# Last inverse transform of a four-layer spectral kernel: row transposes replaced by row products over 32 partitions

## The reference, cut to what matters

```python
x = x + _L0_conv_ref(_gn(x), L0_conv_weights_r, L0_conv_weights_i)
x = x + _L1_conv_ref(_gn(x), L1_conv_gain)
x = x + _L2_conv_ref(_gn(x), L2_conv_weight)
x = x + _L3_conv_ref(_gn(x), L3_conv_weights)
```

```python
x_f = jnp.fft.rfft2(x)
k_f = jnp.fft.rfft2(weights)
out_f = jnp.einsum('bchw,ochw->bohw', x_f, k_f)
out = jnp.fft.irfft2(out_f, s=(H, W))
```

## Time and profile before

| | |
|---|---|
| median of 3 runs | 964.11 us |
| profiled execution, its own time | 966.74 us |
| its span, first to last instruction | 965.0 us |
| granted TensorE clock over the span, mean | 0.933 of full |
| PE busy | 783.1 us (81%) |
| DVE busy | 599.2 us (62%) |
| ACT busy | 517.2 us (54%) |
| POOL busy | 122.3 us (13%) |
| the replaced stage | from about 868.5 us to the end |

### The profile page before, as it was taken

How to read it: one execution, slowest core, us unless ns; L and a number is a source line. 1 busy time by engine, 2 the same in 40 slices (tenths; PEclk the granted TensorE clock), 3 DMA queues, 4 the chain that set the end, 5 groups by cost and what they waited for, 6 DMA issues and landing times. The chain is left out here.

```text
span 965.0 us, 27107 instructions
## 1 busy us (share of the span) xinstructions
PE 783.1 (81%) x10775; PEld 654.0 (68%) x10775; DVE 599.2 (62%) x1112; ACT 517.2 (54%) x868; POOL 122.3 (13%) x120
## 2 busy tenths in 40 slices
PE   5999997872599565787599999985888488979998
PEld 5999996762488443666444444434777488979997
DVE  2454454775847599588777777676666677742222
ACT  0132236863453272565379999004887657765564
POOL 0000000100010054255202222000000100001110
PEclk9999998996899889799799999997999789999999
DMA  6399868542000100000000000004000448831222
GB/s 279 150 373 336 316 203 227 141 98 73 3 1 0 32 9 0 2 0 0 0 2 1 1 1 1 1 1 105 1 0 0 87 89 177 178 81 44 100 106 99
DMA packets 44553, 80.08 MB, mean 83 GB/s; under 512 B 19130, under 2 KB 37568, under 8 KB 40656
## 3 DMA queue, kind: packets, MB, share of 16 engines
q1 hardware_dynamic: 27856, 62.48, 22.7%
q10 hardware_dynamic: 16640, 16.78, 5.1%
HBM read 50.74 MB, written 27.92 MB: 82 GB/s over the span
## 5 line engine op out<-in xcount | busy, mean ns | idle before, releaser
L1473 DVE SCALAR_TENSOR_TENSOR X<-bank,c_power,X 32x512 f32 x128 | 96.8, 757 | 36.4 <-PE bank L1423 32.8
L925 DVE TENSOR_TENSOR X<-X,bank 128x512 f32 x64 | 43.6, 682 | 92.3 <-PE bank L911 92.3
L1616 PE MATMUL bank<-m_xp,m_kf 128*32 128x64 f32 x2048 | 81.6, 246 | 21.9 <-DVE m_xp L1551 10.4
L1616 PEld LDWEIGHTS bank<-m_xp,m_kf 128*32 128x32 f32 x2048 | 80.6, 171 | 23.2 <-issue 23.1
L429 ACT COPY ks_spec<-bank 128x512 f32<-128x512 f32 x64 | 34.3, 589 | 104.1 <-PE bank L357 101.3
L411 DVE COPY ks_rows<-bank 128x512 f32<-128x512 f32 x64 | 41.2, 686 | 72.5 <-PE bank L342 72.5
L215 DVE BATCH_NORM_STATS2 bn<-X 128x6 f32 x128 | 83.1, 683 | 2.9 <-POOL X L1213 1.6
L342 PE MATMUL bank<-ks_fw,ks_src 64*128 64x64 f32 x1024 | 68.7, 298 | 11.4 <-DMA ks_src<-in_L_conv_weights 11.4
L1379 ACT ACTIVATE c_r<-X,c_nrm 32x1024 f32 (+1 forms) x56 | 75.2, 1343 | 2.4 <-DVE c_nrm L1447 1.1
L342 PEld LDWEIGHTS bank<-ks_fw,ks_src 64*128 64x128 f32 x1024 | 68.1, 215 | 11.4 <-issue 11.4
L357 PE MATMUL bank<-ks_fh,ks_rows 64*128 64x128 f32 (+1 forms) x1152 | 72.6, 281 | 0.2 <-ACT ks_spec L429 0.2
(11 more groups left out here) (189 smaller groups left out, 1854.1 us busy)
## 6 DMA issues: line engine op xcount, KB each, us to landing
ks_src<-in_L_conv_weights SPq DMA_DIRECT2D x8, 2048.0 KB, 8.2
kf<-ks_spec ACTq DMA_DIRECT2D x16, 1024.0 KB, 8.7
m_kf<-kf SPq DMA_DIRECT2D x32, 512.0 KB, 8.0
X<-in_x SPq DMA_DIRECT2D x4, 2048.0 KB, 13.7
out_y<-X SPq DMA_DIRECT2D x16, 512.0 KB, 2.6
l_wb<-in_L_conv_weights_r SPq DMA_DIRECT2D x4, 512.0 KB, 11.0
l_wb<-in_L_conv_weights_i SPq DMA_DIRECT2D x4, 512.0 KB, 13.7
xf<-f_xm SPq DMA_DIRECT2D x4, 448.0 KB
```

The lines of the kernel that those rows point to most:

```text
L925: dve.tensor_tensor(x, x, ps[4 + c % 4][:], ALU.add).then_inc(added, 1)
L1473: dve.scalar_tensor_tensor(x, of.rearrange("p (y x) -> p y x", x=HN), filt.power[at, 2:3], x, ALU.mult, ALU.add).then_inc(added, 1)
L1616: last = pe.matmul(ps[4 * half + m // 8][at:at + C, m % 8 * N:(m % 8 + 1) * N], kf[p][:, j, :, H * half + m], xp[half][:, j, m].rearrange( ...
```

## The change

`inverse_stage` is replaced for the last layer by `l3_inverse_stage`, which has no loops and no staging:
- `turn`: 128 transposes read `xm` itself, with a step of 16 elements (64 bytes). VectorE and ScalarE take turns (`turned_by`) in copying four of them at a time to `cols`
- `first_slot`: four small products treat slot 0 (with `l3_first`, which replaces `l3_ih0`), copied back into `cols` by VectorE; then all columns use the one matrix `mh`
- `columns`: 128 products, to banks 0 to 3; results go to `t`, which lies in the memory of `xm`. 20 of the 32 copies are VectorE's, 12 ScalarE's (`made_by`). One product now takes the 4 x 32 columns of all image groups' slots as its stationary operand, so that its result has the slots on the partitions
- pixels: no transposes. For each image row and each of real and imaginary part there are four products, each over 32 partitions (one image group q each), 128 columns of `t` as the stationary operand and 64 moving columns, to bank 4 * (c % 2) + q; real and imaginary part are summed in PSUM. That is 8 chunks of 64 products. VectorE adds four banks to `X` for a chunk, and SyncE stores 256 KB for each, 32 stores in all.

```diff
--- before.py
+++ after.py
@@ -91,7 +91,7 @@
     iw = np.stack([np.cos(ang * np.outer(s, n)), -np.sin(ang * np.outer(s, n))], 1) * 2 / N
     iw[0, 0] = 1.0 / N
     iw[0, 1] = (-1.0) ** n / N
-    out["l3_iw"] = two(iw[sum(SLOT_AT, [])].reshape(2 * SLOT, N))
+    out["l3_iw"] = np.tile(iw[sum(SLOT_AT, [])], (Q, 1, 1)).reshape(P, 2 * N)
     f0 = np.zeros((N, 2, N, 2))
@@ -106,7 +106,7 @@
                 f0[:, half, at, 0], f0[:, half, at, 1] = 1.0, (-1.0) ** n
                 i0[at, 0, :, half], i0[at, 1, :, half] = 1.0 / N, (-1.0) ** n / N
     out["l3_fh0"] = f0.transpose(0, 1, 3, 2).reshape(P, P)
-    out["l3_ih0"] = i0.reshape(P, P)
+    out["l3_first"] = i0.reshape(P, P) @ np.linalg.inv(out["l3_ih"])
     k = np.arange(PS)
@@ -953,6 +953,146 @@
                         if g >= 4:
                             act.wait_ge(pixels, NCH * q + (g - 3) * 4 // per)
                         act.copy(tt[g % 4][:], ps[g % 4][:]).then_inc(turned2_read, 1)
+def l3_inverse_stage(pr, xm, mats):
+    nc, ps = pr.nc, pr.psum
+    SG = SLOT // 4
+    turned, first, first_read, made, pixels, added, stored = (pr.sem(f"i3_{n}") for n in (
+        "turned", "first", "first_read", "made", "pixels", "added", "stored"))
+    turned_read, made_read = ([pr.sem(f"i3_{n}{e}") for e in range(2)] for n in ("turned_read", "made_read"))
+    turned_by = [a % 2 for a in range(SLOT)]
+    made_by = [1 if k % 8 in (1, 4, 7) else 0 for k in range(SLOT)]
+    out_groups = pr.out.rearrange("(q b) c h w -> q (b c) (h w)", b=IB)
+    mh, m0, mw = mats
+    with ExitStack() as ctx:
+        cols = pr.sb(ctx, "i3_cols", [P, IB, C, Q, SLOT])
+        t = xm[:].rearrange("p s k r b -> p (s k r b)").rearrange("p (r h m) -> p r h m", r=2, h=N)
+        def wait_read(eng, sems, by, n):
+            for e in range(2):
+                if e in by[:n]:
+                    eng.wait_ge(sems[e], by[:n].count(e))
+        with nc.Block() as block:
+            @block.sync
+            def _(sp):
+                for c in range(NCH):
+                    for q in range(Q):
+                        sp.wait_ge(added, Q * c + q + 1)
+                        at = slice(c * CH, (c + 1) * CH)
+                        sp.dma_start(out_groups[q][:, at], pr.X[:, q, at]).then_inc(stored, 16)
+                sp.wait_ge(stored, 16 * NCH * Q)
+            @block.tensor
+            def _(pe):
+                def turn(b):
+                    for a in range(SG * b, SG * b + SG):
+                        q, half = a % SG // 2, a % 2
+                        if a >= 4:
+                            wait_read(pe, turned_read, turned_by, a - 3)
+                        for s in range(4):
+                            m = pe.transpose(ps[a % 4][:, s * P:(s + 1) * P],
+                                             xm[:, 4 * half + s, :, :, IB * q + b].rearrange("p k r -> p (k r)"),
+                                             pr.ident[:])
+                        m.then_inc(turned, 1)
+                def first_slot(b):
+                    wait_read(pe, turned_read, turned_by, SG * b + SG)
+                    pe.matmul(ps[4 + b][:, 0:P], m0[:], cols[:, b, :, :, 0].rearrange("p o q -> p (o q)"),
+                              start=True, stop=True).then_inc(first, 1)
+                def columns(b):
+                    pe.wait_ge(first_read, b + 1)
+                    for k in range(SG * b, SG * b + SG):
+                        if k < 4:
+                            wait_read(pe, turned_read, turned_by, SLOT - 3 + k)
+                        else:
+                            wait_read(pe, made_read, made_by, k - 3)
+                        for o in range(4):
+                            m = pe.matmul(ps[k % 4][:, o * P:(o + 1) * P],
+                                          cols[:, b, 4 * (k - SG * b) + o].rearrange("p q s -> p (q s)"), mh[:],
+                                          start=True, stop=True)
+                        m.then_inc(made, 1)
+                turn(0)
+                for b in range(1, IB):
+                    turn(b)
+                    first_slot(b - 1)
+                columns(0)
+                first_slot(IB - 1)
+                for b in range(1, IB):
+                    columns(b)
+                wait_read(pe, made_read, made_by, SLOT)
+                for c in range(NCH):
+                    if c >= 2:
+                        pe.wait_ge(added, Q * (c - 1))
+                    for h in range(ROWS):
+                        for r in range(2):
+                            for q in range(Q):
+                                at = slice(q * SLOT, (q + 1) * SLOT)
+                                m = pe.matmul(ps[4 * (c % 2) + q][:, h * N:(h + 1) * N], t[at, r, ROWS * c + h],
+                                              mw[at, r * N:(r + 1) * N], start=r == 0, stop=r == 1)
+                    m.then_inc(pixels, 1)
+            def copy_turned(eng, copy, e, a):
+                if turned_by[a] == e:
+                    b, q, half = a // SG, a % SG // 2, a % 2
+                    eng.wait_ge(turned, a + 1)
+                    copy(cols[:, b, :, q, 16 * half:16 * half + 16].rearrange("p o (s k) -> p o s k", s=4),
+                         ps[a % 4][:].rearrange("p (s k o) -> p o s k", s=4, k=4)).then_inc(turned_read[e], 1)
+            def copy_made(eng, copy, e, k):
+                if made_by[k] == e:
+                    eng.wait_ge(made, k + 1)
+                    copy(t[:, :, :, 4 * k:4 * k + 4].rearrange("p r h o -> p h r o"),
+                         ps[k % 4][:].rearrange("p (o h r) -> p h r o", o=4, r=2)).then_inc(made_read[e], 1)
+            @block.vector
+            def _(dve):
+                def copy_first(b):
+                    dve.wait_ge(first, b + 1)
+                    dve.tensor_copy(cols[:, b, :, :, 0], ps[4 + b][:, 0:P].rearrange("p (o q) -> p o q", o=C)
+                                    ).then_inc(first_read, 1)
+                for b in range(IB):
+                    for a in range(SG * b, SG * b + SG):
+                        copy_turned(dve, dve.tensor_copy, 0, a)
+                    if b:
+                        copy_first(b - 1)
+                for k in range(SLOT):
+                    if k == SG:
+                        copy_first(IB - 1)
+                    copy_made(dve, dve.tensor_copy, 0, k)
+                for c in range(NCH):
+                    dve.wait_ge(pixels, c + 1)
+                    for q in range(Q):
+                        x = pr.X[:, q, c * CH:(c + 1) * CH]
+                        dve.tensor_tensor(x, x, ps[4 * (c % 2) + q][:], ALU.add).then_inc(added, 1)
+            @block.scalar
+            def _(act):
+                for a in range(SLOT):
+                    copy_turned(act, act.copy, 1, a)
+                for k in range(SLOT):
+                    copy_made(act, act.copy, 1, k)
@@ -1696,7 +1836,7 @@
         if stop == 2: return dump(pr)
         with ExitStack() as layer:
             xm = pr.sb(layer, "xm", [P, SLOT // 4, N, 2, B])
-            inv, inv_loads = matrices(pr, layer, [("l3_ih", [P, P]), ("l3_ih0", [P, P]), ("l3_iw", [P, P])])
+            inv, inv_loads = matrices(pr, layer, [("l3_ih", [P, P]), ("l3_first", [P, P]), ("l3_iw", [P, 2 * N])])
             with ExitStack() as inner:
                 kf0 = pr.sb(inner, "m3_kf0", [P, 2, C, N])
                 loaded = [pr.sem(f"m3_load{p}") for p in range(2)]
@@ -1704,7 +1844,7 @@
                 pr.stats_stage("n3", fwd_loads + inv_loads)
                 l3_forward_stage(pr, fwd, xm, kf0, loaded[0])
                 l3_mix_stage(pr, xm, kf0, loaded)
-            inverse_stage(pr, "i3", xm, SLOT, N, inv, 2, True)
+            l3_inverse_stage(pr, xm, inv)
 def dump(pr):
```

## The result

The changed kernel takes 960.08 us, the median of 15 executions (952.5 to 966.79), against 966.67 us for the kernel before on the same chip (961.53 to 969.58): a ratio of 0.9928 with a 95% interval of 0.9905 to 0.995. That is 0.7% faster where 1.4% was forecast. The profiled execution took 954.41 us with a span of 952.6, close to the 951.1 of the sum; the typical execution is some 6 us longer. The ratio leaves out executions more than 1.5% above the fastest (here one, of 966.79 us).

What follows compares the result with a forecast made beforehand. TensorE, busy almost without a break, was taken to bound the stage. Terms of 17.1 + 28.9 + 0.7 + 30.0 + 2.9 + 3.0 = 82.6 us save 13.9, giving 950.2 us; range 946.9 to 956.8, with starvation 946.5 to 962.

Steps and rivals of the forecast that it cites:

- The sum: Replaced stage: turning, columns, a wait, pixels, adds and last store add to 82.6 us, from 868.5 to 951.1 us.
- first uncertain step: Pixel products: four quarters go on independently past program order, starting four records every 0.112 us, 27.9 ns each.
- The serial rival: Pixel products: records start only behind their predecessors, 55.8 ns each, 57.1 us in all, median 977.3 us; chance 0.17.
- Phase C: Pixel products: 1024 records over 32 partitions in 30.0 us, 3.75 us a chunk, bounds 28.6 to 32.2 us.
- The allowance for the instruction blocks beside the stores: Pixel products: 0.2 us a chunk allowed for what the packet row can't show, giving 3.75 us a chunk.
- The reading of the earlier trace: Instruction blocks: a packet took 1.06 us in quiet, 0.96 us beside 359 GB/s, so the transfer doesn't suffer.
- The starvation rival: Pixel products: stores delay each instruction block to 5 us, making 40 us and a median of 960.2 us; chance 0.15.
- The tail: End of the stage: 0.13 us and four adds, 2.9 us, then 3.0 us from last add to end.
- Turning: Stage's first part: 128 transposes in 16.4 us plus three small first-slot products at 0.224 us, 17.1 us.
- The start: Stage's beginning: TensorE can start at 868.5 us once staging goes, with earlier layers untouched.
- The step that failed: Pixel products: full clock assumed throughout; a half-speed clock, listed as a sign of being wrong, would double the load-bound part.
- The forecast's base: Kernel before: median 964.11 us, from which 13.9 us was taken to give 950.2 us.

Runs made afterwards that it cites:

- the order by pairs: Changed kernel with only the order of its 512 pixel products altered, so neighbours use two quarters of the partitions, not four: 1016.4 us, pixel phase 94.2 us.
- after_f: Changed kernel, unaltered, one more single profile in search of a long execution: 965.73 us, pixel phase 43.3 us.
- the wide kernel: Changed kernel with each pixel product moving 128 columns instead of 64, the second 64 an overwritten copy: medians 956.43, 955.68 and 952.88 us in three sets.

## Why the prediction was wrong

*The sum* named its terms rightly. Its first uncertain step, that quarters go on independently past the program's order, held: four abreast, 0.112 us a step. The serial rival, to which 0.17 was given, is out, though the order by pairs shows what it would have meant.

*Phase C* was mis-sized by 2.0 us in the profiled execution, at the full clock: 32.0 us against 30.0. The allowance for the instruction blocks beside the stores, 0.2 us a chunk, was too small; in six other profiles of the kernel with the clock held the phase took 30.4 to 31.6 us from first to last record, and without stores 28.9 and 29.4. The reading of the earlier trace rows, that a block's packet takes no longer under load, was right but beside the point, since it shows the packet's transfer and not how long it queues. The starvation rival's mechanism is real at a tenth to a quarter of its price of 10 us (1.0 to 2.8 us). On this the Trainium skill ("Runtime: NRT & Kernel Launch", "Instruction fetch mechanics") says "mostly hidden"; 1.9 us of waits in 32 agrees with "mostly", at 28 ns a record. Of the stores, the 395 GB/s put in reach is 408 by its own row, 290 over 0.71; nothing hangs on it.

*The tail* was 6.3 us against 5.9: the adds ran in 2.5 us, but the last store landed later behind three others, 3.8 us from the last add to the end where 3.0 was reckoned.

*Turning* was 0.6 us longer than reckoned, and not for its transposes: all 128 took 16.3 us (9.07, 3.62 and 3.61) against the 16.4 of the sum. Two errors cancel there. The sum gave only the first sixteen transposes the half clock of the earlier trace rows, while in the kernel before the next eight column records still took 1.66 us instead of 0.89, and here the first 64 transposes took 1.8 us more than the rate of the later ones gives. But those came every 0.113 us instead of 0.120. What was mis-sized are the three small products: each held the engine for 0.45 us instead of 0.224. Why is not shown.

*The start* made 1.6 us of the 12.4 between the two profiles by chance. The changed stage itself went from 96.5 to 85.7 us, 10.8 us less, where 13.9 were forecast.

*The step that failed* is one that the sum put at nothing: the full clock through phase C. "A half-speed clock in phase C, which would double its load-bound part" stood among the signs of being wrong, with no chance and no price, and no reason was given for the zero. The rate of phase C came from products over 64 partitions that ran at a granted clock of 1.00; nothing in the trace before had a quarter of the rows. In after_f the clock fell to 0.50 after 14 us of the phase and cost 12 us. It or a shorter form of it is the likeliest cause of the 17 long executions of 49. That is argued and not shown for 16 of them, since only one was profiled; for it are the wide kernel's 0 of 18, and that the scatters of the kernel before and of the wide one are alike, 11.1 and 10.4 us. What sets a fall off is open, and so is why it comes in some executions only.

In the wide kernel, whose profiles show no fall, the median is 954.6 us, 1.1% under the 965.3 of the kernel before in the same three sets, near the forecast's 1.4%. By that comparison the falls take some 4.5 us of the median gain (959.1 less 954.6), an estimate with the chips mixed. The rest of the gap is in the stage at full clock: 3.1 us, of which 2.0 are pixels, 0.6 turning and 0.4 the tail.

The forecast's base was low too: 964.11 us was the median of three executions, and that of fifteen is 966.67. That the median of 960.08 us lies within 946.5 to 962 is no merit of the mechanism, since the top of that range was set by the starvation rival; seven of the first fifteen executions lie above it.

## What to carry to other kernels

When products over 32 partitions ran four abreast, the weight load set the rate, and doubling the moved columns from 64 to 128 cost nothing. It can pay to fill them even with a copy that is overwritten: falls of the clock inside the phase were seen with 64 columns only. Straight-line code at 28 ns a record uses up an instruction block in 3.6 us, so bursts of stores beside it cost; small stores spread out did better than half as many large ones (952.88 us against 957.33 in one set). Compare medians with medians: one profiled execution of a kernel that runs in two ways says little of either's share, and a mean clock over the whole span says little of one stage.

## What was not expected of the hardware

TensorE's granted clock fell while the engine had no idle time: 3.00 of 3.00 us busy before it fell in the order by pairs, and it stayed at 1.2 GHz for the rest of the phase, over 89 us. With the moved columns doubled at the same weight loads the one execution stayed at 2.4 GHz, and the phase took 52.1 us instead of 94.2. Matmuls of other row quarters started ahead of ones that stand before them in the program, at every border of the pairs. The same instructions, four abreast, can run either way: 31 us or 43.3 us. At the lower level a quarter-height load took 328 ns instead of 187, so the load goes with this clock too.
